# Adjacency laid out chunk by chunk in memory, and the own rows' weight blocks made by GpSimd instead of ScalarE

## What is computed

```python
h = jnp.maximum(_layernorm(x), 0.0)
Wh = h @ W
e = leaky_relu((Wh @ a[:128])[:, None] + (Wh @ a[128:])[None, :], 0.2)
mask = (adj > 0) | jnp.eye(N, dtype=bool)
alpha = softmax(where(mask, e, NEG_INF), axis=1)
x = x + alpha @ Wh
...
weights = jnp.where(adj < 1.0, exp(-(1 / adj - 1) ** 2 / 0.5), 0.0)
x = x + weights @ (relu(layernorm(x)) @ W1 + B)
```

## Time and profile before

| | |
|---|---|
| median of three runs | 217.57 us |
| the profiled execution | 217.44 us |
| its span, from the first to the last instruction | 215.6 us |
| busy: VectorE (DVE) | 182.0 us, 84% |
| busy: ScalarE (ACT) | 189.3 us, 88% |
| busy: TensorE (PE) | 154.3 us, 72% |
| busy: GpSimd (POOL) | 132.8 us, 62% |
| moved by DMA | 76.81 MB |
| chain that ended last | DMA 36%, DVE 31%, PE 18% of the span |

### The profile page before, as it was taken

One profiled execution on the slowest core, in us unless ns is written; L12 is line 12 of the kernel. 1 busy time (PEld: TensorE's weight loads), 2 busy tenths in 40 slices (PEclk: granted clock), 3 DMA queues, 4 the chain that ended last, 5 costly groups with the idle time before them and its releaser, 6 DMA issues.

```text
span 215.6 us, 3229 instructions
## 1 busy us (share of the span) xinstructions
PE 154.3 (72%) x956; PEld 103.7 (48%) x970; DVE 182.0 (84%) x535; ACT 189.3 (88%) x207; POOL 132.8 (62%) x140
## 2 busy tenths in 40 slices
PE   0186779983794992989929997499392977799472
PEld 0074565440362760549615844186341654668361
DVE  7993999999979999999488796995986499878855
ACT  0699987599899999999999999799999994999960
POOL 3980002295000588888878888888787788667450
PEclk9999999996599698599985999999979799999995
DMA  5999999999999999999999999999999999961303
GB/s 166 355 413 410 410 408 408 409 411 405 418 418 409 409 393 405 391 400 393 402 388 387 394 401 394 404 387 400 394 387 389 386 401 393 406 229 43 115 23 103
DMA packets 22259, 76.81 MB, mean 356 GB/s; under 512 B 2527, under 2 KB 3126, under 8 KB 22240
## 3 DMA queue, kind: packets, MB, share of 16 engines
q1 hardware_dynamic: 18912, 71.31, 84.7%
q0 software_dynamic: 2912, 5.22, 7.0%
q10 hardware_dynamic: 416, 0.07, 0.2%
HBM read 74.06 MB, written 4.23 MB: 363 GB/s over the span
## 4 chain that ended last, share of the span: by engine, by line
DMA 36%; DVE 31%; PE 18%; issue 7%; ACT 5%; SPq 1%; POOL 1%; POOLq 0%; DVEq 0%
DMA adj_ring<-in_adj 35%; DVE summed L1134 10%; PE bank L642 9%; DVE cand L1172 3%; ACT spread L921 3%; DVE hub_w L1415 3%; PE bank L769 2%; DVE x_sb L1458 2%; PE bank L754 2%; PE bank L761 2%; SPq L383 1%; DMA gathered_rows<-node_table,shared_index 1%; DVE stats L1114 1%; PE bank L629 1%; DVE shared_slots L1230 1%
## 5 line engine op out<-in xcount | busy, mean ns | idle before, releaser
L544 POOL DMA_INDIRECT gathered_rows<-node_table,index x48 | 76.0, 1584 | 36.5 <-DVE index L1309 22.5
L952 ACT ACTIVATE trash_a<-adj_ring,below_one 128x4096 fp8e4<-128x4096 f32 x19 | 70.4, 3705 | 5.7 <-DMA adj_ring<-in_adj 5.2
L642 PE MATMUL bank<-adj_ring,pack_w 128*128 128x512 bf16 (+3 forms) x255 | 70.0, 402 | 2.4 <-DMA adj_ring<-in_adj 1.5
L961 ACT ACTIVATE trash_a<-adj_ring 128x4096 fp8e4<-128x4096 f32 x19 | 68.7, 3614 | 0.5
L1134 DVE SCALAR_TENSOR_TENSOR summed<-adj_ring 128x4096 fp8e4<-128x4096 f32 x13 | 58.0, 4458 | 4.3 <-DMA adj_ring<-in_adj 4.2
L642 PEld LDWEIGHTS bank<-adj_ring,pack_w 128*128 128x128 bf16 x262 | 26.1, 104 | 31.5 <-issue 8.8
L544 POOL DMA_INDIRECT gathered_rows<-node_table,shared_index x24 | 33.2, 1382 | 9.6 <-issue 6.7
L1172 DVE MAX8 cand<-bank 128x8 f32<-128x120 f32 (+25 forms) x82 | 23.3, 351 | 3.9 <-PE bank L642 3.9
L769 PE MATMUL bank<-gathered_rows,spread 128*128 128x129 f32 x160 | 20.9, 282 | 3.9 <-DVE spread L1398 2.4
L769 PEld LDWEIGHTS bank<-gathered_rows,spread 128*128 128x128 f32 x160 | 19.4, 194 | 5.1 <-issue 4.8
L629 PE MATMUL bank<-codes,code_w 128*128 128x512 bf16 x25 | 11.2, 448 | 8.5 <-DMA adj_ring<-in_adj 5.6
(11 more groups left out here) (190 smaller groups left out, 258.4 us busy)
## 6 DMA issues: line engine op xcount, KB each, us to landing
adj_ring<-in_adj SPq DMA_DIRECT2D x32, 2048.0 KB, 23.6
node_table<-gathered_rows POOLq DMA_DIRECT2D x4, 520.0 KB, 8.3
x_sb<-in_x SPq DMA_DIRECT2D x8, 256.0 KB, 5.9
out<-x_sb SPq DMA_DIRECT2D x3, 512.0 KB, 14.2
gathered_rows<-node_table,index POOLq DMA_INDIRECT x48, 5.9
gathered_rows<-node_table,shared_index POOLq DMA_INDIRECT x24, 5.4
out<-x_sb SPq DMA_DIRECT2D x2, 192.0 KB, 2.1
out<-x_sb SPq DMA_DIRECT2D x1, 128.0 KB, 1.9
```

What stands on the lines that cost most here:

```text
L544: pool.indirect_dma_start(out=rows[:, g % RING_GROUPS * GE + t, :], out_offset=None, in_=table, in_offset=bass.IndirectOffsetOnAxis(ap=row ...
L642: last = nc.tensor.matmul(to[:, lo:hi], pack_w[:, k, :], ring_hi[:, i % AR, row_at + lo:row_at + hi], start=False, stop=(k == KB - 1), ski ...
L952: nc.scalar.activation(trash_a[:, :], ring[:, i % AR, :], ACT.Sign, bias=below_one[:, :], scale=-1.0, accum_out=signs[:, n:n + 1], saturat ...
L961: nc.scalar.activation(trash_a[:, :], ring[:, i % AR, :], ACT.Abs, accum_out=sizes[:, n:n + 1], saturate=False).then_inc(checked_a, 1)
```

## The change

The adjacency comes in a second array, laid out on the host before the launch: chunk by chunk, in a chunk partition by partition, so that a partition's four rows of 1024 columns are one piece of 16 KB and a chunk is 2 MB in a row. `load_chunk` reads from it; the general path keeps the old array. The own rows' weight blocks move from ScalarE to GpSimd: in place of eight copies of 128x128 there is one product of 128x1024 for each quarter, the identity times the self weights, ahead of gather groups 0, 3, 6 and 8, behind the same waits. ScalarE's calls are gone. The one of quarter 3 comes just ahead of the three judging steps.

```diff
-OWN_WEIGHTS_AT = {8: 0, 17: 1, 22: 2, CHUNKS: 3}
 ADD_OWN_AT = {13: 0, 21: 1, 29: 2}
 
-def gnn_program(nc, x, adj, w0, a0, w1, b1, out):
+def gnn_program(nc, x, adj, w0, a0, w1, b1, adj_laid, out):
...
-    adj_chunks = adj.rearrange("(s h k p) (c n) -> s c h p k n", s=SG, h=2, k=HK, p=P, n=CW)
...
             def load_chunk(i):
-                s, c, h = chunk(i)
-                sp.dma_start(ring[:, i % AR, :].rearrange("p (k n) -> p k n", k=HK),
-                             adj_chunks[s, c, h]).then_inc(adj_ready[i % AR], 16)
+                sp.dma_start(ring[:, i % AR, :], adj_laid[i]).then_inc(adj_ready[i % AR], 16)
...
+            def own_weights(s):
+                pool.wait_ge(self_set, 1)
+                if s:
+                    pool.wait_ge(own_added, s)
+                blocks = slice(s * KB, (s + 1) * KB)
+                nc.gpsimd.tensor_tensor(own_w[:, :, :],
+                                        ident[:, :].rearrange("p (o n) -> p o n", o=1).broadcast_to([P, KB, P]),
+                                        w_self[:, blocks].rearrange("p (t o) -> p t o", o=1).broadcast_to([P, KB, P]),
+                                        ALU.mult).then_inc(own_w_set, 1)
+
             for g in range(GROUPS):
                 n = PIECE_OF_GROUP[g]
+                if n < SG and g == FIRST_GROUP[n]:
+                    own_weights(n)
                 if g == FIRST_GROUP[HANDED]:
                     judge_checks()
...
-            def own_weights(s):
-                act.wait_ge(self_set, 1)
-                if s:
-                    act.wait_ge(own_added, s)
-                for t in range(KB):
-                    nb = s * KB + t
-                    last = nc.scalar.activation(own_w[:, t, :], ident[:, :], ACT.Copy, scale=w_self[:, nb:nb + 1])
-                last.then_inc(own_w_set, 1)
-
...
-                if i in OWN_WEIGHTS_AT:
-                    own_weights(OWN_WEIGHTS_AT[i])
-                if i == CHUNKS - 1:
-                    own_weights(SG - 1)
...
+def chunks_laid_out(adj, np):
+    laid = np.empty((CHUNKS, P, HK * CW), adj.dtype)
+    for i in range(CHUNKS):
+        s, c, h = chunk(i)
+        planes = adj[s * HR + h * HK * P:s * HR + (h + 1) * HK * P, c * CW:(c + 1) * CW].reshape(HK, P, CW)
+        laid[i] = planes.transpose(1, 0, 2).reshape(P, HK * CW)
+    return laid
...
+    laid = chunks_laid_out(arrays["in_adj"], np)
+    arrays["adj_laid"] = laid
+    args.append(nc.dram_tensor("adj_laid", laid.shape, mybir.dt.from_np(laid.dtype), kind="ExternalInput").ap())
```

## The result

The changed kernel took 228.95 us (median of four runs, 226.84 to 230.74) against 217.07 us for the kernel before (four runs, 216.57 to 217.8): a ratio of 1.051, 95% interval 1.043 to 1.060. It is slower, as forecast, but by some 12 us instead of 2, and the time lies above the range. No shorter execution of the changed kernel has a profile, and this one is 1.8 us above the median.

The account below looks back on a forecast made before the run. GpSimd's gather queue, without slack for 114 us, was taken as the bound. The products' delays, between 1.7 and 2.6 us, were taken as +2.2: 217.44 + 2.2 = 219.6 us, range 214.5 to 224.5.

Parts of the forecast that it names:

- the start of the first gather: GpSimd idles 19.76 us until VectorE has the first indices, then starts gathering at 71.75 us.
- the first product: GpSimd's product ahead of the first gather, hidden in 19.76 us of idle time: sum 0, from -0.2 to +0.5.
- The third rival: Long adjacency pieces hold the gathers up; landing near half way, 5 us more, gives 224.6 us; chance 0.15.
- The queue of GpSimd: 60 gathers with eight checks, without slack for 114 us; later products cost 2.22 us each.
- products 1 and 2: Ahead of gather groups 3 and 6 in GpSimd's full queue: 2 x 2.22 = 4.4 us, moving every gather behind.
- (c): Group 6's gathers issued 4.4 us later plus 3.5 for a check, landed at 179.4: VectorE +2.6 us.
- The products: Four 128x1024 products on GpSimd, 1.92 us each; delays from them give +2.2 us at the end.
- product 3: On GpSimd between gather groups 7 and 8, ahead of judging: 2.2 us, felt only by the gathers behind it.
- The stream: Adjacency loads in 16 KB pieces run 3% faster, 4.9 us at the last chunk.
- the faster rival: The stream's gain reaches the end if GpSimd's queue gives back 4.4 us: 213.3 us; chance 0.18.
- what would show it wrong: GpSimd idle after the first gather, first gather well before 71 us, landings over 8 us, or an end before 216.5.
- near 190: Sign that the forecast is right: GpSimd issues the last gather of group 7 near 190 us.

Follow-up runs that it names:

- short pieces beside the store: The changed kernel with chunks 4 to 10 in pieces of 4 KB, the other 25 in pieces of 16 KB: 220.34 us, ratio 1.013.
- the late start alone: The kernel before with three extra unused 128x1024 products on GpSimd between the first indices and the first gather: 221.93 us, ratio 1.026.

## Why the prediction failed

**The step that failed** is the start of the first gather, held at 71.75: the first product is "Hidden ... Sum 0 (from -0.2 to +0.5)", and the longer pieces cost nothing ahead of the gathers. The prediction took the idle time there as free, and knew of one thing only that ends it, VectorE's indices. There are two, and the second, the table store, had nine us of cover. The change used up all nine and 5.4 more. Those 5.4, and 2.6 of the product that stands behind the same wait, are the 8.0 us by which the first gather is late. The product meets a check there, too: it takes 2.39 us instead of 1.90, the check 6.12 instead of 4.42, the first gather 5.13. That the late start is most of the loss, the runs show without these sums: with short pieces beside the store alone the change takes 220.34 us instead of 228.95.

**The third rival** had the mechanism on the wrong transfer. Long pieces do hold up what shares the engines with them, but the gathers issued from 71 to 187 us land in 6.6 us in the median against 5.9, where it took up to 16.1; the sum of 224.6 us rested on 5 us more.

```profile
DMA to landing us min/median/max: 2.7/6.6/10.3
```

It was the store that went from 11.1 to 24.7: 2 MB that queue for many turns.

**The queue of GpSimd** was read rightly in the main, and the run with the late start alone shows it. The last gather of group 6 ends 12.9 us later (179.96 instead of 167.08): 8.0 from the start, 3.6 from products 1 and 2 with the gaps beside them (two at 1.90; forecast 4.4), and 1.3 from gathers that met checks, since the time of the 52 gathers up to there beyond 1 us each adds up to 29.1 us, before 27.8. This last term isn't a constant: it lies between 21.7 and 30.3 us in the profiles of this document. As forecast in (c), one more check falls ahead of the end of group 6: seven of these gathers are over 2.5 us instead of six, the one at 174.64 among them. Of the 12.9 us VectorE feels 9.4; the other 3.5 is slack, since before it came to group 6 only at 176.78 and never waited.

**Why 5 and 2.5 us make 12.** Slack explains a part. The layout alone delays the end of group 6 by 7.1 us (174.17) and VectorE by 2.7; the products alone delay it by 1.8 (168.91) and VectorE not at all. Together it is 9.4 for VectorE, 6.7 more than the sum. Of these, 2.7 are slack that each change alone uses and both together use once. The other 4.0 arise in the queue, where 12.9 us stand against 7.1 and 1.8: product 0, hidden in the products alone, starts the gathers 1.9 us later than the layout alone does; and the products alone shed 2.8 us of stalls at checks, the change none (smaller gaps beside the products take 0.7 us off again). As two profiles of the layout alone differ by 4 us at this place, the split of the 6.7 us is that of these profiles and no more.

**The products** were priced well as a whole: 219.3 us measured alone, 219.6 forecast. The way there was other than (c): in that kernel the 52 gathers lost 25.0 us instead of 27.8, so 2.8 of the products' 3.8 came back (gaps of 1.1 more took some of it again), and what remained came at groups 7 to 9: VectorE takes group 7 at 192.95 (193.9 forecast), and group 9's first gather starts at 203.96 (204.9 forecast, 203.13 before). One step between them is VectorE's, which writes the indices of group 8 beside product 3 (188.41 to 190.31) in 2.29 us instead of 0.17:

```profile
188.06 2.29 DVE L1307 SCALAR_TENSOR_TENSOR index<-words_i,empty_i 128x8 int32<-128x8 int32 x1
```

That it came near the forecast is thus partly luck. The product itself is 1.90 us; the estimate of 2.25 from the Trainium skill, "GPSIMD Engine Reference", section Performance versus the Vector engine, is too high here.

**The stream** gained as sized: 409 for 395 GB/s is 3.5%, forecast 3%. That it "decides if GpSimd's queue gives back the 4.4 us" was the faster rival's condition; without products and with the store left alone it reaches the end, 2.3 us of it (216.78 - 214.51).

**Behind group 6** the forecast had 2.2 us for product 3, which "only the gathers behind it can feel". The change loses 3.8, and not there. Product 3 waits 2.52 us for the own-row matmuls, a wait that the forecast didn't have, but group 8 starts later than product 3 and the judging end, when VectorE's indices come:

```profile
201.66 1.08 POOL L552 DMA_INDIRECT gathered_rows<-node_table,index  x1 [0.86 <-DVE index L1304]
```

Where VectorE loses them its order in time shows, before and after:

```profile
185.04 1.49 DVE L1172 MAX8 cand<-bank 128x8 f32<-128x24 f32 x5
...
187.62 0.29 DVE L1200 TENSOR_TENSOR placed<-slots,lane_of_p 128x128 f32<-128x128 f32 x1
```

```profile
196.03 1.49 DVE L1167 MAX8 cand<-bank 128x8 f32<-128x24 f32 x5 [1.48 <-PE bank L650]
...
198.61 1.36 DVE L1195 TENSOR_TENSOR placed<-slots,lane_of_p 128x128 f32<-128x128 f32 x1
...
207.92 1.43 DVE L1167 MAX8 cand<-bank 128x8 f32<-128x272 f32 x4 [3.38 <-PE bank L650]
```

It waits 1.48 us for TensorE's words, where it had not waited; a step beside product 3 takes 1.1 us longer; and it waits 3.38 us for words again, instead of 1.47. Against these 4.5 us, the wait of 0.41 for group 7 is gone; that leaves 4.1, near the 3.8. TensorE was late at a lowered clock (below): the columns' matmuls took 3.78 instead of 2.02 us. The last own rows' took 3.81 instead of 2.05 as well. How much of this is the clock's isn't settled.

Of what would show it wrong, the text had GpSimd idle after the first gather and an earlier first gather, not a later one: the very wait that came was on no list. The last gather of group 7 at 190.41, "near 190" as forecast, is luck and no proof of the sum: 8.0 of its 9.4 us of delay are the late start, and one collision with a check that had cost group 7 some 3.5 us moved ahead of it.

## What to carry to other kernels

A longer piece of a stream was paid for here by the other queue on the same DMA engines, since they took turns by packets: look for the largest transfer that shares them, and for what starts when it has landed. An idle stretch has as many ends as the waits that stand in it; list them all, with the time by which each was over, since the trace names the last one alone. Slack at a meeting point and idle time in a queue can be used up once: two changes that each fit into them when measured alone need not add up.

## What was not expected of the hardware

- Two queues share the engines nearly packet for packet at three lengths: 229 to 225 at 4 KB, 213 to 227 at 8 KB, 140 to 142 at 16 KB (the store's packets first). The store's share of the bytes was 49, 31 and 20%.
- Two transfers of half the length per partition left the number of data packets as it was (2,912 and 2,976 with 64 small ones).
- Contiguous chunks in 4 KB pieces gain nothing (216.77 us); the gain lies in the length: 395 GB/s from 116 to 156 us in pieces of 4 KB, 406 in pieces of 8 KB, 409 in pieces of 16 KB.
- GpSimd's product 3 lengthened the VectorE step beside it: 1.36 us instead of 0.29 in the changed kernel, 2.29 instead of 0.17 with the products alone.
- From 178 to 186 us TensorE was busy for 1.11 of 8.00 us at a granted clock of 0.87, and from 186 to 194 the clock stood at 0.50, the lower of its two levels (1.2 of 2.4 GHz), where 16 matmuls took 3.78 us instead of 2.02.
